# Gating stage of a fused layer: ACT and TensorE on groups of different age, the second half in four batches

## The reference, cut to what matters

```
z   = layernorm(ln_c(x))
ab  = sigmoid(z @ gate_w + gate_b) * (z @ lin_w + lin_b) * z_mask
g   = sigmoid(z @ eg_w + eg_b)
blk = einsum('bikc,bkjc->bijc', protein_pair, ab) + einsum('bikc,bjkc->bijc', ab, compound_pair)
x1  = x + g * (layernorm(blk) @ as_w + as_b) * z_mask
logits  = x1 @ Wr + br              # 8 experts
weights = two best of softmax(logits), made to sum to 1
xn  = layernorm(x1)
out = x1 + sum over the two best of weight * (gelu(xe @ W1[e] + b1[e]) @ W2[e] + b2[e])   # xe = xn * ln_g[e] + ln_b[e]
```

## Time and profile before

| | us |
|---|---|
| median of the runs | 1020.41 |
| profiled execution | 1021.31 |
| its span, first to last instruction | 1019.3 |
| TensorE, VectorE, ACT, GpSimd busy in the span | 752.5, 611.3, 583.5, 483.2 |
| gating of half 0, first normalising to the next block products | 123.87 |
| block products of half 1 | 41.76 |
| gating of half 1, to the first scatter's release | 75.78 |
| from there to the first load of the expert stage | 86.98 |
| expert stage | 517.60 |

### The profile page before, as it was taken

One profiled execution on the slowest core, in us unless ns is written; L12 is line 12 of the kernel. 1 busy time (PEld: TensorE's weight loads), 2 busy tenths in 40 slices (PEclk: granted clock), 3 DMA queues, 4 the chain that ended last, 5 costly groups with the idle time before them and its releaser, 6 DMA issues. The chain is left out here.

```text
span 1019.3 us, 24538 instructions
## 1 busy us (share of the span) xinstructions
PE 752.5 (74%) x7306; PEld 647.6 (64%) x7307; DVE 611.3 (60%) x1820; ACT 583.5 (57%) x1157; POOL 483.2 (47%) x539
## 2 busy tenths in 40 slices
PE   2787795655579555542199999999959899899995
PEld 1665695444469544420178878888748788788784
DVE  6556402633752467977077877787736666666663
ACT  2667734655553435341176767767637677667763
POOL 4566400000275720577445656665545555555554
PEclk9989998567689879757599999999989999999998
DMA  7978413644311484412533333333323333333340
GB/s 222 235 231 258 116 32 106 183 125 143 115 56 37 156 251 142 139 56 75 182 98 114 111 119 113 118 117 109 111 85 90 112 106 113 114 116 110 110 123 29
DMA packets 127285, 126.87 MB, mean 124 GB/s; under 512 B 22471, under 2 KB 95454, under 8 KB 127106
## 3 DMA queue, kind: packets, MB, share of 16 engines
q1 hardware_dynamic: 92914, 82.73, 27.9%
q0 software_dynamic: 15296, 34.64, 9.6%
q10 hardware_dynamic: 19024, 8.86, 3.1%
HBM read 79.48 MB, written 49.09 MB: 126 GB/s over the span
## 5 line engine op out<-in xcount | busy, mean ns | idle before, releaser
L967 DVE TENSOR_TENSOR AB<-AB 128x512 f16<-128x512 f32 x280 | 192.3, 687 | 73.9 <-ACT AB L603 68.6
L397 POOL DMA_INDIRECT row_dram<-rows,idx x128 | 127.2, 994 | 203.3 <-DVE rows L775 165.3
L425 POOL DMA_INDIRECT row_dram<-B x140 | 144.0, 1029 | 111.8 <-DVE B L973 77.2
L425 POOL DMA_INDIRECT out<-B x140 | 140.1, 1001 | 116.4 <-DVE B L973 91.1
L600 ACT ACTIVATE AB<-ps 128x512 f16<-128x512 f32 x280 | 168.1, 600 | 41.3 <-PE ps L1155 40.4
L1172 PE MATMUL ps<-PPb,AB 128*128 x1120 | 185.3, 219 | 0.0
L1173 PE MATMUL ps<-PPb,AB 128*128 x1120 | 185.2, 219 | 0.0
L603 ACT ACTIVATE AB<-ps 128x512 f32<-128x512 f32 x280 | 169.1, 604 | 0.0
L1153 PE MATMUL ps<-B,PPb 128*128 128x256 f16 x560 | 154.7, 276 | 0.5 <-issue 0.5
L1154 PE MATMUL ps<-B,PPb 128*128 128x256 f16 x560 | 154.3, 276 | 0.0
L1155 PE MATMUL ps<-B,PPb 128*128 128x256 f16 x560 | 154.3, 275 | 0.0
(11 more groups left out here) (201 smaller groups left out, 1483.7 us busy)
## 6 DMA issues: line engine op xcount, KB each, us to landing
B<-row_dram SPq DMA_DIRECT2D x70, 264.0 KB
B<-row_dram SPq DMA_DIRECT2D x70, 136.0 KB
rows<-in_x SPq DMA_DIRECT2D x32, 256.0 KB, 5.0
rows<-in_L_conv_protein_pair SPq DMA_DIRECT2D x16, 512.0 KB, 4.3
g_dram<-work ACTq DMA_DIRECT2D x32, 256.0 KB, 3.1
work<-g_dram SPq DMA_DIRECT2D x32, 256.0 KB, 2.7
ABT<-in_x SPq DMA_DIRECT2D x32, 256.0 KB, 3.0
ABT<-in_L_conv_protein_pair SPq DMA_DIRECT2D x16, 512.0 KB, 4.0
```

The costliest lines, as they stand in the source:

```text
L397: pool.indirect_dma_start(row_dram, bass.IndirectOffsetOnAxis(ap=idx[:, j:j + 1], axis=0), rows[:, j, :], None).then_inc(scattered[b], 16)
L425: pool.indirect_dma_start(out_rows if second else row2_dram, bass.IndirectOffsetOnAxis(ap=Rw[:, u, b, at:at + 1].bitcast(u32), axis=0), Rw ...
L967: dve.tensor_tensor(Hp[:, hs, 1, :], Hf[:, q, :], Hp[:, hs, 0, :], ALU.subtract).then_inc(h_parts[q], 1)
```

## The change

The lags in by_step change, on ACT and on TensorE, and with them the steps of the extra work. ACT's list becomes logit_copy 7, norm_b 0, bT_copy 2, x1T_copy 5, pp_copy1 2; TensorE's becomes bT 1, as_mm 3, x1T_mm 4, logit 6. Half 1 has four batches of 16 columns. `choose` is cut into three functions, two_best, count and places, which stand behind different gates; VectorE computes x1_spread and x1_scales of the next batch between them. The statistics of half 1 have a place of their own (in AB), so that they can stand beside the arrays of a running choice.

```diff
-BATCHES = ((0, 0, 32), (0, 32, NC), (1, 0, 32), (1, 32, 48), (1, 48, NC))
+BATCHES = ((0, 0, 32), (0, 32, NC), (1, 0, 16), (1, 16, 32), (1, 32, 48), (1, 48, NC))
...
-        x1m = work[:, 1024:1184].rearrange("p (v j) -> p v j", v=5)
-        x1v, x1q, x1r, x1t = (work[:, 1184 + 64 * k:1248 + 64 * k] for k in range(4))
+        x1own = (work[:, 1024:1440], AB[:, :, :, :].rearrange("p h c j -> p (h c j)")[:, 6656:7072])
...
             set_keep(16, 1)
             scatter(2)
             scatter(3)
-            pool.wait_ge(s.tail_done, 5)
+            scatter(4)
+            pool.wait_ge(s.tail_done, 6)
...
-            scatter(4)
+            scatter(5)
...
-                then = {4: [lambda: b_root(h, 1)], 10: [lambda: x1_root(2 * h)], 13: [lambda: weights(2 * h)]}
+                then = {4: [lambda: b_root(h, 1)]}
                 if h:
-                    then.update({14: [lambda: x1_root(3)], 17: [lambda: weights(3)], 18: [lambda: x1_root(4)]})
+                    then.update({7: [lambda: x1_root(2)], 11: [lambda: weights(2), lambda: x1_root(3)],
+                                 15: [lambda: weights(3), lambda: x1_root(4)], 19: [lambda: weights(4), lambda: x1_root(5)]})
                 else:
-                    then.update({18: [lambda: x1_root(1)]})
-                by_step(GH, [(0, norm_b), (1, bT_copy), (3, x1T_copy), (4, logit_copy), (0, pp_copy1)], then)
+                    then.update({11: [lambda: x1_root(0)], 16: [lambda: weights(0)], 19: [lambda: x1_root(1)]})
+                by_step(GH, [(7, logit_copy), (0, norm_b), (2, bT_copy), (5, x1T_copy), (2, pp_copy1)], then)
...
-                    if n == 7:
-                        x1_spread(2 * h)
-                    if n == 10:
-                        x1_scales(2 * h)
-                    if n == 11:
-                        choose(2 * h)
-                        if h:
-                            x1_spread(3)
-                    if n == 14 and h:
-                        x1_scales(3)
+                    if h:
+                        b, k = 2 + n // 4, n % 4
+                        if k == 3:
+                            if b > 2:
+                                choose(b - 1, (0,))
+                            x1_spread(b)
+                        elif k == 0 and b > 3:
+                            choose(b - 2, (1,))
+                        elif k == 1 and b > 2:
+                            x1_scales(b - 1)
+                        elif k == 2 and b > 3:
+                            choose(b - 2, (2,))
+                    elif n == 7:
+                        x1_spread(0)
+                    elif n == 9:
+                        x1_scales(0)
+                    elif n in (12, 13):
+                        choose(0, (n - 12,))
+                    elif n == 15:
+                        choose(0, (2,))
 
                 by_step(GH, [(0, gate_b)])
                 if h:
-                    choose(3)
-                x1_spread(4 if h else 1)
-                x1_scales(4 if h else 1)
-            choose(4)
+                    choose(4, (1,))
+                    x1_scales(5)
+                    choose(4, (2,))
+                else:
+                    x1_spread(1)
+                    x1_scales(1)
+            choose(5)
...
-                then = {13: [lambda: ranks(2 * h)]}
                 if h:
-                    then[17] = [lambda: ranks(3)]
-                by_step(GH, [(0, bT), (1, as_mm), (3, x1T_mm), (4, logit)], then)
+                    then = {12: [lambda: ranks(2)], 16: [lambda: ranks(3)], 21: [lambda: ranks(4)]}
+                else:
+                    then = {17: [lambda: ranks(0)]}
+                by_step(GH, [(1, bT), (3, as_mm), (4, x1T_mm), (6, logit)], then)
```

More of the change, by code:

```diff
@@ L128, in build @@
         x1st = sb("x1st", [P, NC, 6])
-        x1m = work[:, 1024:1184].rearrange("p (v j) -> p v j", v=5)
-        x1v, x1q, x1r, x1t = (work[:, 1184 + 64 * k:1248 + 64 * k] for k in range(4))
+        x1own = (work[:, 1024:1440], AB[:, :, :, :].rearrange("p h c j -> p (h c j)")[:, 6656:7072])
+        x1ms = [a[:, 0:160].rearrange("p (v j) -> p v j", v=5) for a in x1own]
+        x1vs, x1qs, x1rs, x1ts = ([a[:, 160 + 64 * k:224 + 64 * k] for a in x1own] for k in range(4))
         half = sb("half", [P, XB * TG])
@@ L517, in x1_root @@
                 nj = BATCHES[b][2] - BATCHES[b][1]
-                act.activation(x1q[:, 0:2 * nj], x1v[:, 0:2 * nj], ACT.Sqrt).then_inc(s.x1_root, 1)
+                h = BATCHES[b][0]
+                act.activation(x1qs[h][:, 0:2 * nj], x1vs[h][:, 0:2 * nj], ACT.Sqrt).then_inc(s.x1_root, 1)
             for h in range(IC):
@@ L706, in _, with tail, choose @@
                     {3: [first_weights], 7: [second_weights]})
-            def choose(b):
+            tails = [0]
+            def tail(i):
+                i.then_inc(s.tail, 1)
+                tails[0] += 1
+                dve.wait_ge(s.tail, tails[0])
+            def choose(b, parts=(0, 1, 2)):
                 h, j0, j1 = BATCHES[b]
@@ L712, in choose, with two_best @@
                 c = choices[nj]
[L713 to L718, removed]
+                for part in parts:
+                    (two_best, count, places)[part](b, h, j0, j1, nj, c)
+            def two_best(b, h, j0, j1, nj, c):
+                assert tails[0] == TAIL * b, tails
                 over = lambda a, shape: a.rearrange("p (t o) -> p t o", o=1).broadcast_to(shape)
@@ L743, in choose, with count @@
                 tail(dve.tensor_tensor(c.m12[:, DL, :], c.m12[:, DL, :], c.m12[:, LT, :], ALU.mult))
-                gj = [P, NG, nj]
+            def count(b, h, j0, j1, nj, c):
+                over = lambda a, shape: a.rearrange("p (t o) -> p t o", o=1).broadcast_to(shape)
                 ej = [P, NE, nj]
@@ L756, in choose, with places @@
                 dve.tensor_scalar(c.base, IG[:, :], float(CAP), -1.0, ALU.mult, ALU.add)
+            def places(b, h, j0, j1, nj, c):
+                over = lambda a, shape: a.rearrange("p (t o) -> p t o", o=1).broadcast_to(shape)
+                gj = [P, NG, nj]
                 sh, dv = (rows[:, j0:j1, q:q + 1].rearrange("p j o -> p (j o)") for q in (SH, RS))
@@ L815, in x1_spread @@
             def x1_spread(b):
[L816 removed]
+                h, j0, j1 = BATCHES[b]
                 nj = j1 - j0
[L818 removed]
+                m, v = x1ms[h][:, :, 0:nj], x1vs[h]
                 spread(x1st[:, j0:j1, :], m, D)
[L820 to L821 removed]
+                dve.tensor_scalar(v[:, 0:nj], m[:, 0, :], 1.0 / D, 1e-5, ALU.mult, ALU.add)
+                dve.tensor_scalar(v[:, nj:2 * nj], m[:, 0, :], (1.0 + 1e-5) / D, 1e-10, ALU.mult, ALU.add).then_inc(s.x1_var, 1)
             def x1_scales(b):
[L824 removed]
+                h, j0, j1 = BATCHES[b]
                 nj = j1 - j0
+                r = x1rs[h][:, 0:2 * nj]
                 dve.wait_ge(s.x1_root, b + 1)
[L827 removed]
+                inverse(x1vs[h][:, 0:2 * nj], x1qs[h][:, 0:2 * nj], r, x1ts[h][:, 0:2 * nj])
                 dve.tensor_scalar(rows[:, j0:j1, R1:RS + 1].rearrange("p t v -> p v t"),
[L829 to L830 removed]
+                                  r.rearrange("p (v t) -> p v t", v=2), 1.0, None, ALU.mult)
+                bstep(dve.tensor_scalar(rows[:, j0:j1, SH:SH + 1].rearrange("p t o -> p (t o)"), x1ms[h][:, 1, 0:nj], 0.5, None, ALU.mult))
             for h in range(IC):
```

6 lines of the change are left out of this document (3 added, 3 removed).

## The result

The changed kernel took 988.82 us (median of 4 runs, 984.08 to 992.93), beside 1021.61 us of the kernel before on the same chip: a ratio of 0.9669 [0.9606, 0.9732]. The forecast was 981.3, range 973 to 998. The profiled execution took 991.6 us, its span 988.9.

A forecast was written before the change was run, and what follows sets the result against it. In the first half's gating no engine is full: ACT and TensorE wait for each other, 8.37 us a step. 1021.3 - 31.7 - 7.6 + 0.2 = 982.2 us profiled, less 0.9: 981.3, range 973 to 998.

The forecast's parts named there:

- The step: First half's gating: a steady step costs the larger of ACT and TensorE, 4.2 us, instead of their sum, 8.37.
- The head: Start of the first half's gating: copies stand behind square root and scales, putting gate 3 at 24.3 us, gate 4 at 32.3.
- To gate 12 and the choice: First half: groups 4 to 12 at 4.2 us reach 65.9; the cut choice with gates and spread takes 23.3, to 89.2.
- The drain: End of the first half's gating: the second batch's square root, then two rounds of logits, about 3 us, ending at 92.2.
- The block products: Block products of the second half: they keep their order and their 41.76 us.
- The second half: Second half's gating to the first release: VectorE's work 50.9 us plus idle time, 68.2 in all, 7.6 gained.
- Four batches: Release to the expert stage's first load: GpSimd waits at most 0.2 us between batches; 86.98 stays, 0.2 lost.
- A: Rival, both gating halves: TensorE stays at the lower clock level, adding 13.2 us, time 994.5; chance 0.09.
- B: Rival, first half's gating: the loads become the bound, costing some 10 us, time 991; chance 0.06.
- C: Rival, first half: an unseen wait keeps the engines' old circle, only the second half gains 7.4, time 1013; chance 0.04.
- D: Rival, the 64 scatters: busy VectorE holds GpSimd's descriptors, one microsecond more each, 64 us, time 1045; chance 0.04.

The follow-up runs named there:

- e1_lags: The kernel before with only the new lags of ACT and TensorE, batches and uncut choose as before: 990.75 us, ratio 0.9692.
- e6_half_pairs: The changed kernel with ACT's first-half copies of protein_pair cut to half of their rows: 979.82 us, ratio 0.9593.
- e3_head: The changed kernel with 32 instead of 24 columns of statistics ahead and the others' square root two steps later on ACT: 966.38 us, ratio 0.9451.
- e4_drain: The changed kernel with the first half's square root for the second batch three steps later, behind the last copies: 981.97 us, ratio 0.9591.

## Why the prediction was right, point by point

- **The step.** Forecast 4.2 us with ACT as the bound; measured 4.04, ACT without a gap. e1_lags has the gain without the rest, e6_half_pairs shows that ACT sets it.
- **The head.** Gates 3 and 4 were forecast 24.3 and 32.3 us into the stretch, behind waits of 3.8; they stand at 24.76 and 33.09, behind 4.41 and 4.29. e3_head removed their cause.
- **To gate 12 and the choice.** Forecast 65.9; measured 64.42 (243.79). The second batch's spread was to end at 89.2; ACT's square root behind it starts at 267.20, 87.83 in.
- **The drain** was undersized: 3 us, measured 271.95 - 267.20 = 4.75. The first half came to 92.58 against 92.2, since these errors cancel.
- **The block products** were to keep 41.76 and took 42.52. TensorE comes out of a 4.95 us wait behind the square root, the last two rounds of logits take 2.05 us each and its first transposes run partly at the lower level, 16 in 3.26 us (granted clock 0.50 from 267.68 to 271.95, 0.63 up to 275.20, then 1.00); in e1_lags, where the three rounds of logits just ahead took 1.13 each, eight take 1.04 and the stretch is 41.76.
- **The second half.** Forecast 68.2, measured 70.18. VectorE's work is 50.67 (forecast 50.9). Its idle time is 19.5, forecast 17.3: 6.93 at the first gate (6.5), 4.41 and 3.29 at the head (6.8), 1.44 at gate 5 that was not forecast. Of the 5.6 us won, 4.1 are work taken from ahead of the release (forecast 3.9) and only 1.5 idle time (forecast 3.7), so the waits for as_mm paid for less than I had thought.
- **Four batches.** A gap of 0.57 between the first two (forecast at most 0.2), the stretch 87.40 against 87.18.
- **Rivals.** A: TensorE's granted clock was 0.81 in the first half, above 0.66 as forecast, but 0.76 in the second, below the 0.84 that I gave as the mark. It cost little there: behind gate 5 VectorE waits for no as_mm before the release. The Trainium skill (TensorE: Matmul & The Clock Gate, "Loop structure matters more than you think") tells of matmuls that wait for long and then run at half clock, and by it I had expected the second half to be the colder one. The trace agrees, 0.76 against 0.81. B: loads at a share of 0.81 were near, not the bound. C: the engines came apart. D: a scatter took 1009 ns with VectorE busy for 64.68 of 87.40 us, 1006 ns with 54.08 of 86.98, so the fuller VectorE did not make them dearer. Single scatters are stretched all the same, before and after, as the last section shows; over the 64 it is some 3 us (64.5 - 64 x 0.96). The Trainium skill (SBUF — State Buffer, "SBUF: two separate sides") tells of VectorE instructions that lock GpSimd out. The trace agrees in kind in these scatters; whether they are of the kind that the Trainium skill names, no row shows.

The profiled execution lay 9.4 us above the 982.2 of the sum: 6.06 from the input stage, 0.4 from the first half, 0.8 from the block products, 2.0 from the second half, 0.2 to the load, 0.7 outside the span, less 0.75 in the expert stage. The largest is no term of the change: I took one profiled run's 173.31 for a property of the kernel before, and it was the early end of what the same program does. The four stretches themselves sum to 292.68 against 328.39, 35.7 less where the terms gave 39.1: 3.4 us too hopeful.

## What to carry to other kernels

When two engines hand work to each other in turn, the step costs their sum until each takes work that the other finished a step earlier; then look at what stands in the longer chain's head and tail, since an instruction that waits for a third engine (here a square root for VectorE's variances) holds up everything that is queued behind it, and moving two such roots by two and three steps (with eight more columns ahead) took off another 25 to 28 us, beside the change's 33. A shorter chain ahead of a release is worth its length only if what follows is fed as fast: try such an edit in the surrounding in which it will live. A gain can also be hidden by a wait behind it, as the cut choice's 4.6 us in the first half were by a square root. Take a stage's length from more than one profiled run before it becomes a base of the sum.

## What the runs showed of the hardware

The input stage of the same program ended at 172.8 to 175.4 us in seven profiled runs, and at 178.5 to 181.3 in six, nothing between. The two kinds part in the window from 60 to 90 us; the kernel before, first run:

```profile
60.00:90.00 30.00, 23.25 (x122) 18.38 (x120) 18.49 (x87) 22.42 (x34) 17.64 (x29) 1.00 0.83 256
```

and its second run:

```profile
60.00:90.00 30.00, 23.71 (x106) 17.96 (x107) 15.65 (x77) 19.66 (x32) 17.78 (x31) 0.89 0.71 217
```

In the seven the core moved 246 to 259 GB/s there at a granted clock of 0.99 to 1.00, in the six 211 to 218 at 0.89 to 0.94. What decides it stays open: the clock may follow from late loads as well as the other way round. No experiment was made on it.

Most scatters on GpSimd take 0.95 or 0.96 us. In the changed kernel seven of the 64 take more than 1.1, up to 1.66. Each of the seven started while VectorE was in one of a few instructions (L766, L785, L871, L968, L972) and ended 0.77 to 0.85 us after that instruction did, as if most of the scatter's work had waited for it. The longest beside its VectorE instruction, which ends at 456.89:

```profile
456.07 1.66 POOL L399 DMA_INDIRECT row_dram<-rows,idx  x1 [0.30 <-issue]
...
455.68 1.21 DVE L972 TENSOR_TENSOR AB<-AB 1x1024 f32<-1x1024 f32 x1
```

Scatters that started in a gate's first instruction, which reads PSUM (L867, at 384.90, 400.76 and 406.28), took 0.95 to 0.96 us, and so did the last seven, from 461.26 on, with VectorE idle. So it depends on what VectorE does at the moment at which a scatter starts, more than on how busy VectorE is. The mean was 993 to 1027 ns over all runs; in e4_drain, with the highest, ten scatters took more than 1.1 us.
